# Layer 0 of a four-layer graph network: run sums as one product a block, the root on VectorE, end positions shifted by a product

## The chip, the cores and the metric

The kernel runs on one core of a Trainium2 chip. The metric is the device time of one execution in microseconds. A core has five engines: TensorE (PE; its weight loads are shown as PEld), VectorE (DVE), ScalarE (ACT), GpSimd (POOL) and SyncE (SP), which here only issues DMAs. Each engine runs its own instructions in order; between engines they wait on semaphores.

## What is computed

Four graph layers one after the other on 3125 nodes of 128 features and 103,125 edges, sorted by destination. The change touches the first, an attention over the edges of each destination node:

```python
q_dst = Q[dst] + rel_q[edge_type]
k_src = K[src] + rel_k[edge_type] + (time_emb @ Wt + bt)
v_src = V[src] + rel_v[edge_type]
euclid = sum(q_dst * k_src, axis=-1) / sqrt(DH)          # 8 heads of 16
decay = exp(decay_scale * tanh(relu(dec_in @ Wd1 + bd1) @ Wd2 + bd2))
man_dist = norm(m[src] - m[dst])                         # m: nodes mapped into a ball
logits = (alpha * euclid - (1 - alpha) * hyp_beta * man_dist) * decay
ex = exp(logits - segment_max(logits, dst)[dst])
agg = segment_sum(v_src * ex, dst) / segment_sum(ex, dst)
out = agg @ Wo + bo                                      # then norm, feed-forward, norm
```

## The kernel before

**Tiles and blocks.** Edges are cut into tiles of 128 and blocks of 8 tiles (`TPB`), 101 blocks (`NBLK`), 808 tiles (`TT`). One edge of a tile lies on each partition. Since edges are sorted by destination, a tile's edges fall into runs of equal destination. A node's edges may go on from one tile into the next.

**The layer-0 loop.** `sp_l0_windows`, `pool_l0_windows`, `act_l0_windows`, `dve_l0_windows` and `pe_l0_windows` are the five engines' programs of one software pipeline of `NBLK + 3` turns. In turn n they work on block n (loads, decay), block n-1 (scores and logits), block n-2 (run maxima, exponentials) and block n-3 (messages and sums). The order on each engine is written out by hand; semaphores of `Signals` (`g.…`) join them. A flag from the data (`all_near`) picks this path, since each block's destinations lie within 126 nodes (`WIN`).

**GpSimd** gathers the 128 source rows of 384 floats for each tile by indirect DMA (`pool_gather`, L1200) into a ring of four block buffers `GS`, eight gathers a block. For block n it first waits until `GS` of block n-4 is used (`gs_used`). Ahead of the seventh gather of turn n it takes the root of the squared distances of block n-2 (`pool_w_distances`, L1238): 128x8 elements to the power 0.5.

**SP** loads for each block the window of destination rows, the near keys, decay inputs, edge attributes, run rows (L916) and destination keys as two bf16 rows (L908), and stores the block's sums, 8 tiles x 128 rows x 144 floats, into `y_rows` (L921).

**TensorE** makes for each half block the attribute addend (L2451) and the picked destination rows (`pe_w_products`, L2459), turns logits into rows and back (L2479, L2495, L2496), spreads the keys over partitions (`pe_same_half`, L2420), and multiplies for each tile the matrix `same` (edge e and edge f have one destination) with the messages (`pe_sums`, L2443 and L2444), so that each of a tile's 128 rows holds its run's sum. In the trace an fp32 product is two records. The four pairs of a block's sums are spread over the turn. `pe_keep_busy` (L2434) makes three products of 128x512 into bank 0 that nothing reads.

**VectorE**, in its order: positions work (below), messages (L1870), scores of the first half (L1880, L1882, L1884), the decayed logits and two scans over runs (L1916 to L1922), `same` of the first half (L1854), scores of the second half, `same` of the second half, the head reduction (L1931), the window's low part (L1890), and then, after GpSimd's root (`dist_ready`), the logits (L1938 to L1940).

**ScalarE** makes the pick weights (L1411, L1418), the squares with their sums (L1394), the decay's functions, the exponentials, and copies the sums out of PSUM, four times 128x272 a block (L1380).

**End positions.** `dve_positions` finds for each node where its edges end, as a generator that is advanced once a turn: 25 turns with two 808-wide instructions each (L1823, L1824), then 25 turns in which GpSimd gathers a row of keys (a ninth gather) and VectorE counts in it (L1830, L1831). Then the end positions go to DRAM and come back shifted by one node, as start positions (`sp_positions`, L967 to L972, the third and fourth DMA column-wise in 4-byte pieces), for which VectorE waits at L1839.

**After the loop** `sp_join` loads the last row of each tile, `pool_join` gathers for each node the row of its last edge (`end_ix`) and the carry of its tile (`tile_ix`), and the join adds what earlier tiles hold of a node.

## Time and profile before

| | us |
|---|---|
| median of 3 runs | 4303.54 |
| lowest and highest of them | 4303.48 and 4307.41 |
| the profiled execution's own time | 4303.84 |
| its span, first to last instruction | 4302.1 |
| mean granted TensorE clock | 0.891 |

| engine | busy us | share of the span | instructions |
|---|---|---|---|
| TensorE products | 3349.1 | 78% | 31445 |
| TensorE weight loads | 2746.6 | 64% | 31445 |
| VectorE | 3220.5 | 75% | 6328 |
| ScalarE | 2083.6 | 48% | 6017 |
| GpSimd | 2220.2 | 52% | 2554 |

The layer-0 loop lies between about 190 and 1530 us of the span. The rest is the preparation ahead of it and the other three layers behind it, which the change leaves as they are. In the rows below a time is in us from the span's start; "mean ns" is that of one record; "[2.56 <-POOL …]" says how long the engine was idle before the instruction and what ended that. The share of busy time is an average over all layers; what a change in the loop is worth is read from the loop's own rows. The granted clock is given as a share of the full one, 2.4 GHz; the other level is 1.2 GHz.

### The profile page before, as it was taken

What the parts mean: (1) busy time and instruction counts of PE and PEld (TensorE: products, weight loads), DVE (VectorE), ACT (ScalarE), POOL (GpSimd) and SP (SyncE); (2) the same over time, 40 slices, a digit from 0 to 9 for tenths busy, and PEclk for the clock granted to TensorE, in tenths of its full rate; (3) what the DMA queues carried; (4) which work ended last, traced back from release to release, by engine and by line L of the source; (5) the groups of instructions that cost most, each with busy time, mean ns of one, the idle gap of its engine ahead of it and who ended that gap; (6) DMA issues with size and microseconds to landing.
All of it is one profiled execution on the core that took longest, in us unless ns stands there. A gap on an engine that the chain in (4) does not pass through costs nothing.

```text
span 4302.1 us, 86569 instructions
## 1 busy us (share of the span) xinstructions
PE 3349.1 (78%) x31445; PEld 2746.6 (64%) x31445; DVE 3220.5 (75%) x6328; ACT 2083.6 (48%) x6017; POOL 2220.2 (52%) x2554
## 2 busy tenths in 40 slices
PE   1389889879999936177856788857899999779995
PEld 1155555545555524177745678744899999679995
DVE  5488877767777734799957887767666666779997
ACT  2366655546666613499944576730322222234443
POOL 0277788858888750088822200000455555458883
PEclk7699999989999968588877899978999999989998
DMA  4677777778888720100002211123344444223331
GB/s 89 212 208 216 211 207 209 206 162 232 229 228 229 216 67 1 42 13 14 13 10 95 80 40 48 40 100 117 114 129 124 127 122 128 85 68 128 127 128 66
DMA packets 387384, 524.58 MB, mean 122 GB/s; under 512 B 85571, under 2 KB 315269, under 8 KB 386815
## 3 DMA queue, kind: packets, MB, share of 16 engines
q1 hardware_dynamic: 332799, 354.60, 27.8%
q0 software_dynamic: 54144, 164.25, 14.2%
q8 instruction: 258, 4.23, 0.4%
q14 instruction: 183, 1.50, 0.1%
HBM read 407.61 MB, written 111.07 MB: 121 GB/s over the span
## 4 chain that ended last, share of the span: by engine, by line
PE 33%; DVE 24%; POOL 21%; issue 11%; ACT 5%; DMA 4%; SPq 2%; DVEq 0%; POOLq 0%; ACTq 0%
POOL arena_a L1200 16%; PE psum L3726 5%; POOL arena_c L1238 4%; PE psum L3742 4%; PE psum L3677 4%; PE psum L3675 4%; PE psum L3642 2%; PE psum L3701 2%; PE psum L3724 2%; PE psum L3314 2%; DVE arena_a L3222 2%; PE psum L3673 2%; DVE arena_c L3215 1%; DVE msg_parts L3464 1%; DVE Hn L3192 1%
## 5 line engine op out<-in xcount | busy, mean ns | idle before, releaser
L1200 POOL DMA_INDIRECT arena_a<-src_table,src_tix x808 | 832.2, 1030 | 429.6 <-issue 387.8
L3446 POOL TENSOR_SCALAR node_hot<-arena_c 128x128 fp32r<-128x128 f32 x575 | 365.4, 646 | 903.3 <-DVE arena_c L3334 566.8
L3464 DVE SCALAR_TENSOR_TENSOR msg_parts<-psum,msg_parts 128x512 fp32r<-128x512 f32 (+2 forms) x644 | 425.6, 661 | 259.4 <-ACT msg_parts L3613 226.4
L3164 POOL TENSOR_SCALAR node_hot_dst<-arena_c 128x128 fp32r<-128x128 f32 x587 | 382.2, 667 | 123.9 <-DVE arena_c L3568 67.9
L3613 ACT ACTIVATE msg_parts<-psum 128x512 fp32r<-128x512 f32 (+2 forms) x325 | 186.2, 573 | 520.6 <-PE psum L3677 520.6
L3675 PE MATMUL psum<-arena_c,arena_a 128*128 128x128 bf16 x3675 | 406.4, 220 | 0.0
L3677 PE MATMUL psum<-arena_c,arena_a 128*128 128x128 bf16 x3675 | 406.4, 220 | 0.0
L1394 ACT ACTIVATE arena_a<-arena_a 128x128 f32<-128x128 f32 x808 | 239.2, 297 | 195.5 <-DVE arena_a L1882 195.3
L3673 PE MATMUL psum<-src_tix,arena_a 128*128 128x128 bf16 x1225 | 272.4, 222 | 71.0 <-DVE arena_a L3350 37.2
L3042 PE MATMUL psum<-arena_a,arena_c 128*128 128x150 f32 x1800 | 291.3, 329 | 39.9 <-ACT arena_c L2984 39.7
L3628 ACT ACTIVATE msg_parts<-psum 128x512 fp32r<-128x512 f32 (+1 forms) x319 | 185.2, 581 | 260.4 <-PE psum L3726 260.4
L3042 PEld LDWEIGHTS psum<-arena_a,arena_c 128*128 128x128 f32 x1800 | 280.5, 222 | 45.1 <-ACT arena_c L2984 43.8
L3726 PE MATMUL psum<-arena_c,arena_a 128*128 128x128 bf16 x3675 | 308.9, 219 | 0.0
L2434 PE MATMUL psum<-weights,ident 128*128 128x512 f32 x606 | 279.1, 597 | 0.1
L3314 PE MATMUL psum<-arena_a,arena_c 128*128 128x129 f32 x1250 | 201.1, 307 | 84.9 <-DVE arena_c L3215 84.8
L2981 ACT ACTIVATE arena_c<-arena_c,arena_b 128x128 f32<-128x128 f32 x850 | 251.1, 386 | 28.5 <-DVE arena_b L2895 28.5
L3675 PEld LDWEIGHTS psum<-arena_c,arena_a 128*128 128x128 bf16 x3675 | 258.1, 98 | 0.0
L1380 ACT ACTIVATE arena_c<-psum 128x272 f32<-128x272 f32 x404 | 157.5, 390 | 207.8 <-PE psum L2444 201.8
L3726 PEld LDWEIGHTS psum<-arena_c,arena_a 128*128 128x128 bf16 x3675 | 258.0, 98 | 0.0
L2443 PE MATMUL psum<-arena_c 128*128 128x136 f32 x808 | 186.8, 314 | 91.1 <-DVE arena_c L1870 91.0
L3677 PEld LDWEIGHTS psum<-arena_c,arena_a 128*128 128x128 bf16 x3675 | 257.7, 98 | 0.0
L2443 PEld LDWEIGHTS psum<-arena_c 128*128 128x128 f32 x808 | 135.7, 198 | 183.3 <-DVE arena_c L1870 111.4
(599 smaller groups left out, 10095.6 us busy)
## 6 DMA issues: line engine op xcount, KB each, us to landing
y_rows<-arena_c SPq DMA_DIRECT2D x101, 576.0 KB, 4.2
arena_a<-bucket_rows SPq DMA_DIRECT2D x150, 384.0 KB
arena_b<-near_keys SPq DMA_DIRECT2D x101, 252.0 KB
arena_a<-bucket_rows SPq DMA_DIRECT2D x50, 448.0 KB
arena_a<-bucket_lists SPq DMA_DIRECT2D x25, 896.0 KB
pair_counts<-arena_c SPq DMA_DIRECT2D x25, 800.0 KB
arena_a<-bucket_lists SPq DMA_DIRECT2D x25, 704.0 KB
arena_a<-src_table,src_tix POOLq DMA_INDIRECT x808
```

The lines of the kernel that those rows point to most:

```text
L1200: e.indirect_dma_start(out_, None, table, bass.IndirectOffsetOnAxis(ap=idx, axis=0)).then_inc(sem, 16)
L2434: e.matmul(bank[0][:, :], ident[:, :], Wt4[:, :], start=True, stop=True)
L2443: e.matmul(bank[bk][:, 0:w], same[s][:, t, :], msg[s][:, t, 0:w], start=True, stop=True)
L3042: put = e.matmul(bank[2 + s][:, 0:3 * KT], hot_pos[s][:, j, :], routed_v[s][:, j, :, :].rearrange("p f k -> p (f k)"), start=(j == 0), sto ...
L3164: return e.tensor_scalar(node_hot3[at % RING_H][:, i, :], iota_row, dst_lo[:, b, t:t + 1], None, ALU.is_equal)
L3314: put = e.matmul(bank[6 + b % 2][:, 0:D + 1], expd[b % 2][:, k, :], H1[:, k, :], start=(k == 0), stop=(k == NB - 1))
L3446: return e.tensor_scalar(node_hot[at % RING_M][:, i, :], iota_row, src_lo[:, b, 2 * k + j:2 * k + j + 1], None, ALU.is_equal)
L3464: e.scalar_tensor_tensor(out=to[:, 1, 0:nt, :], in0=bank[at % 4][:, 0:nt * P].rearrange("p (t f) -> p t f", f=P), scalar=0.0, in1=to[:, 0, ...
L3673: e.matmul(to, attr_rows[s][:, c_], Wc12, start=True, stop=False)
L3675: e.matmul(to, row_hot[0][s][:, c_], A3[:, part, sb_ * D:(sb_ + 1) * D], start=False, stop=False)
L3677: put = e.matmul(to, row_hot[1][s][:, c_], B3[:, part, b * D:(b + 1) * D], start=False, stop=(part == 2))
L3726: put = e.matmul(to, src_rows3[s][:, c_], A3[:, part, k * D:(k + 1) * D], start=False, stop=(part == 2))
```

## The change

- **Root.** `pool_w_distances` is gone from GpSimd. VectorE starts from a first guess taken from the bits of the number, and makes two Heron steps (guess + d2/guess) with two reciprocals, on 128x8 elements; its constants are folded into the next multiply. GpSimd's wait for a free ring buffer is now on the squares.
- **Run sums.** A block's nodes get rows by their number modulo 112 (`RES` = 128 - 16), so that a whole block's sums come from one accumulated product group: eight products of 128x144 into one bank (`pe_run_sums`), one copy out of PSUM (`act_run_sums`), and two stores (`sp_store_runs`), of 120 and of 8 rows of 144 floats. Rows 112 to 119 take the runs that carry over from an earlier tile (one for each tile), the last 8 rows the run at the end of each tile. The matrix for it (`dve_run_rows`) compares row numbers from `row_col` and `last_col`, made once ahead of the loop (`dve_run_columns`, with four products that shift the destination column by one partition or take its last one). The run's maximum goes in as 8 further columns, masked to the run's first edge (`first_col`). The key loads, `pe_same_half` and `dve_same_half` go from this loop.
- **End positions.** The shift by one node is a product with a rotated identity (`rotated`) and copies out of PSUM, instead of DMAs to DRAM and back. Index arithmetic for `run_ix` is added behind it. The gathers of end rows and the loads of last rows move into the loop's functions (`pool_end_rows`, `sp_last_rows`), behind the same waits.
- **Unread products.** `pe_keep_busy` is gone.
- The flag asks for a reach below 112 instead of 126 nodes, from the block's unclamped first key.

```diff
-                        e.wait_ge(g.dist_ready, n - RING + 1)
+                        e.wait_ge(g.squares, 2 * (n - RING + 1))
                     for t in range(TPB):
-                        if t == 3 * TPB // 4 and n >= 2:
-                            pool_w_distances(e, n - 2)
                         pool_gather(e, GS[n % RING][:, t, :], src0, src_tix[:, n * TPB + t:n * TPB + t + 1], g.d_gs[n % RING])
-                elif n - 2 < NBLK:
-                    pool_w_distances(e, n - 2)
+            pool_end_rows(e, 0, 1, 1, run_sums, run_ix)
...
+        def sp_store_runs(e, k):
+            s = k % 2
+            e.wait_ge(g.sums_out, 4 * (k + 1))
+            e.dma_start(run_sums[k * RES_ALL:(k + 1) * RES_ALL, :], sums_w[s][0:RES_ALL, :]).then_inc(g.d_y[s], 16)
+            e.dma_start(last_sums[k * TPB:(k + 1) * TPB, :], sums_w[s][RES_ALL:P, :]).then_inc(g.d_last[s], 16)
...
+        def act_run_sums(e, k):
+            s = k % 2
+            e.wait_ge(g.sums_pe, 4 * (k + 1))
+            if k >= 2:
+                e.wait_ge(g.d_y[s], 16 * (k // 2))
+                e.wait_ge(g.d_last[s], 16 * (k // 2))
+            e.activation(sums_w[s], bank[SUM_BANKS_W[s]][:, 0:WMAX], ACT.Copy).then_inc(g.sums_out, 4)
...
         def dve_l0_messages(e, k):
             s, r = k % 2, k % RING
             e.wait_ge(g.exp_ready, k + 1)
+            e.wait_ge(g.max_copied, k + 1)
             if k >= 2:
                 e.wait_ge(g.sums_pe, 4 * (k - 1))
-            e.tensor_tensor(msg[s][:, :, 0:D].rearrange("p t (h w) -> p t h w", h=H),
+            e.tensor_tensor(msg_w[s][:, :, D + H:D + 2 * H], v3(max_w[s]), bc(first_col[:, k * TPB:(k + 1) * TPB], 2, H), ALU.mult)
+            e.tensor_tensor(msg_w[s][:, :, 0:D].rearrange("p t (h w) -> p t h w", h=H),
...
+        def dve_run_rows(e, k):
+            s = k % 2
+            if k >= 2:
+                e.wait_ge(g.sums_pe, 4 * (k - 1))
+            at = slice(k * TPB, (k + 1) * TPB)
+            e.tensor_tensor(same[s][:, :, 0:RES_ALL], bc(row_col[:, at], 2, RES_ALL), bc(row_no_w[:, 0:RES_ALL], 1, TPB), ALU.is_equal)
+            e.tensor_tensor(same[s][:, :, RES_ALL:P], bc(last_col[:, at], 2, TPB), bc(row_no_w[:, RES_ALL:P], 1, TPB), ALU.is_equal).then_inc(g.same_ready, 2)
...
-                    dve_same_half(e, i2, 0, dst_col, 0)
+                    dve_run_rows(e, i2)
                 if b1:
                     dve_w_scores(e, i1, 1)
-                if b2:
-                    dve_same_half(e, i2, 1, dst_col, 0)
-                if b1:
                     eu, d2, lg, t1 = small[s1][:, 0, :], small[s1][:, 1, 0:TPB], small[s1][:, 3, :], small[s1][:, 4, :]
                     e.wait_ge(g.q_used, 2 * i1 + 2)
                     own.mark(e.tensor_reduce(v3(eu), GS[i1 % RING][:, :, 0:D].rearrange("p t (h w) -> p t h w", h=H), AX, ALU.add))
+                    guess, other = small[s1][:, 1, TPB:2 * TPB], small[s1][:, 1, 2 * TPB:3 * TPB]
+                    e.wait_ge(g.squares, 2 * i1 + 2)
+                    own.step(e.tensor_scalar(guess.bitcast(I32), d2.bitcast(I32), 0.5, ROOT_BITS, ALU.mult, ALU.add))
+                    own.mark(e.reciprocal(other, guess))
                 if b0:
                     dve_w_low(e, i0)
                 if b1:
-                    e.wait_ge(g.dist_ready, i1 + 1)
+                    own.settle()
+                    own.mark(e.tensor_tensor(other, other, d2, ALU.mult))
+                    own.mark(e.tensor_tensor(v3(eu), v3(eu), bc(hrow[:, 1, :], 1, TPB), ALU.mult))
+                    own.settle()
+                    own.step(e.tensor_tensor(guess, guess, other, ALU.add))
+                    own.step(e.reciprocal(other, guess))
+                    own.step(e.tensor_tensor(other, other, d2, ALU.mult))
+                    own.step(e.scalar_tensor_tensor(out=guess, in0=guess, scalar=0.25 * ROOT_TRIM ** 2, in1=other, op0=ALU.mult, op1=ALU.add))
                     if i1 >= 2:
                         e.wait_ge(g.rows_pe, i1 - 1)
-                    own.step(e.tensor_tensor(v3(t1), bc(d2, 2, H), bc(hrow[:, 2, :], 1, TPB), ALU.mult))
-                    own.step(e.tensor_tensor(v3(eu), v3(eu), bc(hrow[:, 1, :], 1, TPB), ALU.mult))
+                    own.step(e.scalar_tensor_tensor(out=v3(t1), in0=bc(guess, 2, H), scalar=1.0 / ROOT_TRIM, in1=bc(hrow[:, 2, :], 1, TPB), op0=ALU.mult, op1=ALU.mult))
                     e.tensor_tensor(lg, eu, t1, ALU.subtract).then_inc(g.logits_ready, 1)
...
-        def pe_keep_busy(e, k):
-
-            e.wait_ge(g.addend_used, 2 * k + 2)
-            for _ in range(3):
-                e.matmul(bank[0][:, :], ident[:, :], Wt4[:, :], start=True, stop=True)
-
...
+        def pe_run_sums(e, k):
+            s = k % 2
+            e.wait_ge(g.gs_used, k + 1)
+            e.wait_ge(g.same_ready, 2 * (k + 1))
+            if k >= 2:
+                e.wait_ge(g.sums_out, 4 * (k - 1))
+            for t in range(TPB):
+                rows = e.matmul(bank[SUM_BANKS_W[s]][:, 0:WMAX], same[s][:, t, :], msg_w[s][:, t, :], start=(t == 0), stop=(t == TPB - 1))
+            rows.then_inc(g.sums_pe, 4)
...
                 if b3:
-                    e.wait_ge(g.gs_used, i3 + 1)
-                    pe_sums(e, i3, D + H, 0, 0, SUM_BANKS_W)
+                    pe_run_sums(e, i3)
...
+                if n == 2 * NB + 1:
+                    e.wait_ge(g.pos_ends, 1)
+                    e.matmul(bank[2][:, 0:NB], keys_pos[True][1], end, start=True, stop=True).then_inc(g.d_pos, 48)
```

## Rows read from the trace of the kernel before

**Rows 1.** Chain of waits by line, 1000 to 1030 us, steady part.

```profile
by line: POOL arena_a L1200 64.3%; issue 27.8%; POOL arena_c L1238 11.2%
```

**Rows 2.** Stretches: length, power instruction's busy (count), clock, DMA share, GB/s.

```profile
209.90:521.40 311.50, 43.30 (x24) 0.96 0.76 210
521.40:868.40 347.00, 41.91 (x25) 0.91 0.74 206
868.40:946.40 78.00, 6.67 (x4) 0.74 0.71 144
946.40:1495.30 548.90, 75.33 (x45) 1.00 0.81 228
```

**Rows 3.** Timeline, GpSimd: start, duration us, operation [idle before <- releaser].

```profile
1007.26 1.67 POOL L1238 TENSOR_TENSOR arena_c<-arena_c,weights 128x8 f32<-128x8 f32 x1
1009.11 1.02 POOL L1200 DMA_INDIRECT arena_a<-src_table,src_tix  x1 [0.18 <-issue]
...
1011.97 0.95 POOL L1200 DMA_INDIRECT arena_a<-src_table,src_tix  x1 [0.30 <-issue]
```

**Rows 4.** Timeline, VectorE, same window: parts of one block.

```profile
1008.97 0.23 DVE L1938 TENSOR_TENSOR arena_c<-arena_c,hrow 128x64 f32<-128x64 f32 x1 [2.56 <-POOL arena_c L1238]
1009.48 0.22 DVE L1940 TENSOR_TENSOR arena_c<-arena_c 128x64 f32<-128x64 f32 x1
1009.63 1.22 DVE L1870 TENSOR_TENSOR arena_c<-arena_a,arena_c 128x1024 f32<-128x1024 f32 x1
1010.76 0.68 DVE L1880 TENSOR_TENSOR arena_a<-arena_a,psum 128x512 f32<-128x512 f32 x1
...
1012.55 0.28 DVE L1916 TENSOR_TENSOR arena_c<-psum,arena_c 64x128 f32<-64x128 f32 x1
...
1014.16 0.68 DVE L1854 TENSOR_TENSOR arena_c<-psum,dst_col 128x512 f32<-128x512 f32 x1
```

**Rows 5.** VectorE's waits, 872 to 945: us, times, longest us.

```profile
DVE npos L1839 <- DMA npos<-end_pos: 12.5, 1, 12.5
DVE arena_c L1916 <- DMA arena_c<-run_rows: 12.5, 2, 12.3
```

**Rows 6.** Timeline, VectorE, before the loop: 25-wide waited steps.

```profile
44.67 0.18 DVE L1711 TENSOR_SCALAR stat<-stat 128x25 f32<-128x25 f32 x1
44.88 0.31 DVE L1712 RECIPROCAL stat<-stat 128x25 f32<-128x25 f32 x1
```

**Rows 7.** Groups by line, VectorE, 211 to 520: busy us, mean ns.

```profile
L1824 DVE TENSOR_REDUCE npos<-arena_b 128x1 f32<-128x808 f32 x24 | 23.9, 995 | 0.8
L1823 DVE TENSOR_SCALAR arena_b<-dst_tix,node_id 128x808 f32<-128x808 f32 x24 | 15.2, 633 | 0.0
```

**Rows 8.** Stretch before the loop: length, VectorE busy (count), clock, DMA.

```profile
176.20:191.50 15.30, 0.00 (x0) 0.50 0.79 213
```

**Rows 9.** The page's groups by line: busy us, mean ns, idle before.

```profile
L2434 PE MATMUL psum<-weights,ident 128*128 128x512 f32 x606 | 279.1, 597 | 0.1
```

**Rows 10.** One block: PE, PEld, DVE, ACT, POOL busy (counts), clock, DMA.

```profile
1009.60:1021.90 12.30, 11.45 (x58) 7.27 (x56) 9.57 (x20) 8.12 (x30) 9.97 (x10) 1.00 0.80 227
```

**Rows 11.** Chain of waits at the loop's end: start us, us, what.

```profile
1524.11 0.45 PE psum L2443 x2
...
1529.09 4.62 DMA y_rows<-arena_c
```

**Rows 12.** Timeline, TensorE, at three places in order of time.

```profile
306.36 0.50 PE L2443 MATMUL psum<-arena_c 128*128 128x136 f32 x2 [1.72 <-DVE arena_c L1870]
...
941.27 2.69 PE L2459 MATMUL psum<-win_parts_last,pick_w_last 128*128 128x256 f32 x8
...
1010.90 0.50 PE L2443 MATMUL psum<-arena_c 128*128 128x136 f32 x2 [0.82 <-DVE arena_c L1870]
...
1012.10 1.12 PE L2451 MATMUL psum<-weights,arena_c 128*128 128x512 f32 x2
1012.78 1.40 PE L2459 MATMUL psum<-win_parts_last,pick_w_last 128*128 128x256 f32 x8
```

More of the change, by code:

```diff
@@ L54 @@
 WIN = P - NET
+RES = P - 2 * TPB
+RES_ALL = RES + TPB
+ROUND = 8388608.0
 def bc(ap, axis, n):
@@ L502, in program @@
         tlog = [c_.take(4 * P, TPB * H).rearrange("p (t f) -> p t f", t=4) for _ in range(2)]
+        runs_at = 2 * TPB * P
+        w_at = runs_at + 2 * TPB * WMAX
+        flat_c = lambda at, n: arena_c[:, at:at + n]
+        msg_w = [flat_c(runs_at + s * TPB * WMAX, TPB * WMAX).rearrange("p (t f) -> p t f", t=TPB) for s in range(2)]
+        sums_w = [flat_c(w_at + s * WMAX, WMAX) for s in range(2)]
+        row_col, last_col, first_col = (flat_c(w_at + 2 * WMAX + i * TT, TT) for i in range(3))
+        row_no_w = flat_c(w_at + 2 * WMAX + 3 * TT, P)
+        max_w = [flat_c(w_at + 2 * WMAX + 3 * TT + P + s * TPB * H, TPB * H) for s in range(2)]
+        shift_w, final_w = same[0][:, 0, :], same[0][:, 1, :]
+        no_edge = same[0][:, 2, 0:1]
+        run_t = [flat_c(TPB * P, TT), flat_c(runs_at, TT), flat_c(runs_at + TT, TT)]
         RING_IX = 3
@@ L963, in sp_positions @@
             e.dma_start(last_row, row_bc(first_last[1, 0:TT])).then_inc(g.d_pos, 16)
+            if near:
+                return
             for _ in range(2 * NB + 2):
@@ L1838, in dve_positions @@
             e.wait_ge(g.d_pos, 80)
+            if near:
+                e.wait_ge(g.pos_ends, 1)
+                own.mark(e.tensor_copy(start[:, 1:NB], bank[2][:, 1:NB]))
+                own.step(e.tensor_copy(start[:, 0:1], bank[2][:, 0:1]))
+                own.mark(e.tensor_copy(start[0:1, 1:NB], bank[2][0:1, 0:NB - 1]))
+                own.step(e.memset(start[0:1, 0:1], 0.0))
             own.step(e.tensor_tensor(degree, end, start, ALU.subtract))
@@ L1846, in dve_positions @@
             own.step(e.tensor_tensor(has_carry, has_carry, valid, ALU.mult))
+            if not near:
+                return
+            own.mark(e.tensor_scalar(run_ix[:, :], tile_ix[:, :], 3, None, ALU.arith_shift_right))
+            own.step(e.tensor_scalar(lastp, node_id[:, :], 1.0 / RES, 0.5 / RES - 0.5, ALU.mult, ALU.add))
+            own.mark(e.tensor_copy(cnt, run_ix[:, :]))
+            own.step(e.tensor_scalar(lastp, lastp, ROUND, None, ALU.add))
+            own.step(e.tensor_scalar(lastp, lastp, -ROUND, None, ALU.add))
+            own.mark(e.scalar_tensor_tensor(out=start, in0=cnt, scalar=-float(TPB), in1=te, op0=ALU.mult, op1=ALU.add))
+            own.step(e.scalar_tensor_tensor(out=lastp, in0=lastp, scalar=-float(RES), in1=node_id[:, :], op0=ALU.mult, op1=ALU.add))
+            own.step(e.scalar_tensor_tensor(out=start, in0=start, scalar=float(RES), in1=lastp, op0=ALU.add, op1=ALU.subtract))
+            own.step(e.tensor_tensor(start, start, has_carry, ALU.mult))
+            own.step(e.tensor_tensor(lastp, lastp, start, ALU.add))
+            own.step(e.scalar_tensor_tensor(out=run_ix[:, :], in0=cnt, scalar=float(RES_ALL), in1=lastp, op0=ALU.mult, op1=ALU.add))
         def dve_same_half(e, k, hf, key_col, layers):
@@ L1895, in dve_l0_windows @@
             e.tensor_tensor(minus_place, minus_place, iota_col, ALU.subtract)
-            e.memset(half_row, 0.5)
             e.memset(wd2_wide, 0.0)
+            e.memset(shift_w[:, 0:1], 0.0)
+            e.tensor_copy(shift_w[:, 1:P], ident[:, 0:P - 1])
+            e.tensor_scalar(final_w, ones[:, :], ident[:, P - 1:P], None, ALU.mult)
+            own.mark(e.tensor_scalar(no_edge, ident[:, 0:1], -5.0, None, ALU.mult))
             e.memset(wd1_2, 0.0).then_inc(g.l0_prep, 1)
+            dve_run_columns(e, own)
             positions = dve_positions(e, own, True)
@@ L2464, in pe_l0_windows @@
             rows_ = bank[3][0:R, 0:P]
+            e.wait_ge(g.l0_prep, 2)
+            for i, (lo, hi) in enumerate(((0, HALF), (HALF, TT))):
+                e.matmul(bank[1 + 6 * i][:, 0:hi - lo], shift_w, dst_col[:, lo:hi], start=True, stop=True)
+                columns = e.matmul(bank[2 + 4 * i][:, 0:hi - lo], final_w, dst_col[:, lo:hi], start=True, stop=True)
+            columns.then_inc(g.keys_read, 2 * NBLK)
             e.wait_ge(g.d_dec, 192)
```

108 lines of the change are left out of this document (66 added, 42 removed).

## The prediction

> **What bounds the kernel now.** I read the views in this order: the chain of waits, the layer-0 loop in stretches, then one block of it on each engine. In the steady part of the loop the chain lies on GpSimd alone: gathers of source rows, the issue gaps between them, and the power instruction [rows 1]. The loop goes through four stretches, cut at the starts of that instruction: 24 blocks in 311.5 us (12.98 each), 25 in 347.0 (13.88), 4 in 78.0 (19.5), 45 in 548.9 (12.20) [rows 2]. In the last, GpSimd never waits for another engine; the power instruction takes 1.67 us and the next gather starts 0.18 after it, where a gather follows a gather after 0.30 [rows 3]. VectorE meanwhile stands idle 2.56 us before L1938, waiting for it [rows 4]. In the 24 blocks VectorE also does two 808-wide instructions for the end positions, in the 25 GpSimd does a ninth gather. In the 4 blocks VectorE waits 12.5 us for the start positions that come back from DRAM and 12.5 for a load of run rows queued on SP behind them [rows 5].
>
> **GpSimd.** Without the power instruction a block loses 1.67 + 0.18 - 0.30 = 1.55 us: its floor falls to 12.20 - 1.55 = 10.65, and to 13.88 - 1.55 = 12.33 where it has nine gathers. The ring of four buffers gives a gather about two block times, so it isn't what binds. The gathers of end rows only move to another function, same place in the queue. One small iota is put ahead of the first gather: at most 1 us, in GpSimd's slack while VectorE is late.
>
> **VectorE** is next late, so its block must be priced, in start-to-start steps [rows 4]. A 1024-wide instruction costs 1.13, a 64-wide one 0.15, or 0.26 if the next waits for it (0.51 for two). The block is then: the new masked maximum, 64 wide, 0.15; messages 1.13; scores of the first half 1.79; the scans 1.61; the new comparison for the whole block, 960 and 64 elements, 1.06 + 0.15 = 1.21 in place of two of 512 (0.60 each); scores of the second half 1.79; reduction 1.13. That is 8.81. The root comes on top. A 25-wide step with a wait costs 0.21, a reciprocal 0.35 [rows 6]; for 8 elements I take 0.20 and 0.25. First guess 0.20, reciprocal 0.13 (the window's low part runs in its shadow, 256 wide and so between the 64 and the 512: 0.33), product and scaled score 0.35, then add, reciprocal, product, weighted sum 0.20 + 0.25 + 0.20 + 0.20, the two 64-wide ones 0.25 + 0.15. With the low part that is 2.26, so 11.07 a block. The bounds of the root: 0.5 less if waits hide in each other, and 0.9 more if each of its seven waited steps costs the 0.35 of a reciprocal. It now waits for ScalarE's squares where GpSimd did; behind the wait stand the guess, the low part and the logits, and TensorE's next picks wait for the low part. The second multiply and the reduction (0.60 + 1.13) lie between, so I take 0, at most 0.5. In the 24 blocks the position work adds 0.63 + 1.00 and two gaps [rows 7], 1.70, so 12.77; in the 25, two 128-wide ones, about 0.5, so 11.57, under GpSimd's 12.33.
>
> Before the loop about 18 VectorE instructions of 400 to 808 elements and four products are added. At 0.65 to 1.0 us each and some 6 us for the products they take about 13 us, inside a stretch of 15.3 us in which VectorE does nothing [rows 8]. I take 0; if that cover were short, the overrun counts in full, 5 us at most.
>
> **TensorE.** Removed per block: the three unread products (L2434, 279.1 us over 101 blocks, 2.76 each [rows 9]) and the two key products. The engine was busy 11.45 of 12.30 [rows 10], so it is left with about 8 of 11 to 13 us. The other edit is in the order. The sums were spread, one pair ahead of the second half's picks; now all eight stand ahead of them. From the end of the messages at full clock: eight products at 0.23 (half of the 0.45 that one takes at the low clock [rows 11]) and 0.1 to start, 1.94; the hidden product about 0.3; the addend 0.68 and the picks 1.40 [rows 12]. Ready after 4.3 us. VectorE wants them after 1.79 + 1.61 + 1.21 + 0.60 = 5.2, so 0.9 is left. At the low clock it is 3.7 (eight at 0.45 and the start) + 0.5 + 1.36 (twice 0.68) + 2.69 [rows 12] = 8.25: VectorE then stalls 3.0 us.
>
> The granted clock therefore decides the size. In the steady stretch TensorE waits 0.82 us a block for the messages and stays at 1.00, which is 2.4 GHz; with 1.7 us of waiting the mean is 0.96 [rows 2, 12], so some time passes at 1.2 GHz. After the change it idles from the end of its decay and addend products, some 9.2 us after a block's low part, until the next low part at 11.1, and again until the messages are done: 1.9 + 1.0 us, in the 24 blocks 1.9 + 2.8. I expect a low spell in most blocks, over part of the sums and picks only, since the engine is full again once they run: 3.6 us of them in the 24 blocks, where it idles longest, 2.4 otherwise (estimates). A low spell costs half its length, 1.8 and 1.2. Less the 0.9 this leaves a stall of about 0.9 us in the 24 blocks, 0.3 later; bounds 0 and 3.0.
>
> The Trainium skill speaks against the change here ("TensorE: Matmul & The Clock Gate", section "HAM oscillation — how this bites in real kernels"): a loop whose TensorE waits in each turn can lose the high clock in each turn. Were every block's second half run at the low clock, it would give the slower rival below instead of the forecast.
>
> **ScalarE and DMA.** Four evictions of 272 columns become one of 144; the store of 576 KB a block becomes 74 KB in two issues, the 4 KB key load goes. Nothing waited for these in the steady stretch, so 0. ScalarE's new wait, for the block's sums, ends about 2 us after the messages and holds back the squares of the second half, which can't start for another 4: 0.
>
> **End positions.** The round trip through DRAM goes, for one product, two copies and some 15 steps of 25 elements (about 4.5 us with the index arithmetic). The 4 blocks become 4 x 11.37 + 4.5 = 50.
>
> **The end.** The last sums are one run instead of four, and the last store and its landing (4.62 us [rows 11]) shrink: I take 6 us, between 2 and 9.
>
> **The sum**, against the profiled execution's own 4303.84 us (its span is 4302.1; the median of the three runs is 4303.54, 0.3 less, which I neglect):
> 24 x (12.77 + 0.9) = 328.1, +16.6; 25 x 12.33 = 308.3, -38.7; 50 for 78, -28.0; 45 x (11.07 + 0.3) = 511.7, -37.2; the end -6. Together -93.3: **4210 us**.
>
> **Rivals.**
> - *The clock holds.* The gaps are short, as is the 0.82 at full clock [rows 12]. Stalls 0: 24 x -0.21, -39, -29, 45 x -1.13, -6, that is -130: 4174. If moreover GpSimd's gathers drop to the 0.95 + 0.30 of a plain one [rows 3], the nine-gather stretch falls to 11.57: 4155.
> - *The root is dear.* 0.9 us more on 98 blocks, less what GpSimd covers in the 25: about +65, 4275. For it: each step is a round trip on one engine. Against: [rows 6].
> - *TensorE binds, slower.* The low clock covers the stretch from the sums to the second picks in most blocks. With a mean stall s above 0.74 us the sum is -149 + 98 s; it turns slower at s = 1.5, half of the 3.0. With s = 2.0: +47, 4351. For it: the unread products are gone and the sums now stand in front. Against: a busy stretch brings the clock back, since the 1.00 of the steady stretch followed a stretch of 0.74 [rows 2].
> - *The cover is elsewhere*: VectorE's growth eats what GpSimd gives up (11.07 + 1.1 a block), only the round trip stays: about -5 to +10, 4305.
>
> **How the numbers follow.** Forecast 0.5 (4180 to 4245), clock holds 0.22, dear root 0.13, TensorE binds 0.08, no gain 0.05, below all 0.02. The range takes the first three with the root's upper bound: 4150 to 4285. Faster by over 0.2% (8.6 us, about what a measurement can tell from no change): 0.87; within 0.04; slower 0.09.
>
> **What would show it.** No power instruction; VectorE's idle before L1938's successor gone and VectorE at 95% or more of the loop; block times near 13.7, 12.3 and 11.4; TensorE's clock in the last stretch below 1.00, with VectorE's waits in front of the second half's subtraction naming the picks; no wait for end_pos. The prediction is wrong if the waited 8-wide steps aren't near 0.20, if the low clock covers all or none of the sums, or if the work before the loop sticks out of its 15.3 us.

## The result, and the profile after

The changed kernel takes 4260.4 us (median of 4 runs, 4251.7 to 4263.3), the kernel before beside it 4305.5 (4 runs, 4303.5 to 4309.7): a ratio of 0.9891, interval 0.9873 to 0.9908, 45 us or 1.1% faster. The forecast was 4210, 93 us faster. The sign is right, less than half of the size came. Submitted again later on another chip (after_again, below), it took 4262.6 us in three of five executions; the other two, 4354.5 and 4356.4 us, fell in a slower state that some executions show, and count in no ratio here.

The page of the changed kernel, its span, parts 1 and 2 (engines, clock and DMA in 40 slices), the engines' shares of the chain, and two of the groups by line:

```profile
span 4261.3 us, 84541 instructions
PE 3127.8 (73%) x30647; PEld 2694.0 (63%) x30647; DVE 3368.9 (79%) x7173; ACT 1961.6 (46%) x5714; POOL 2053.6 (48%) x2454
...
POOL 0355567776666440288813200000555555368883
PEclk7688889899999857688867899978999999889998
DMA  4755566666666410100012211133444444223331
...
PE 42%; DVE 41%; issue 7%; ACT 5%; DMA 3%; SPq 2%; POOL 1%; DVEq 0%; ACTq 0%; POOLq 0%
...
L1232 POOL DMA_INDIRECT arena_a<-src_table,src_tix x808 | 829.9, 1027 | 411.8 <-issue 224.9
...
L2567 PE MATMUL psum<-arena_c 128*128 128x144 f32 x1616 | 327.8, 378 | 156.1 <-DVE arena_c L1926 156.1
```

The power instruction is gone, and with it GpSimd's place in the chain of waits (1%): it now waits for VectorE to free a ring buffer. These shares are of the whole span, all four layers. Of the chain between 210 and 520 us alone the run sums (L2567) take 27%: TensorE now bounds a part of this loop. The loop's four stretches, as columns us, then PE, PEld, DVE, ACT and POOL busy, granted clock, DMA share and GB/s, and what VectorE waits for in the loop:

```profile
210.00:520.00 310.00, 223.86 (x1021) 165.85 (x1020) 271.98 (x625) 145.93 (x558) 165.32 (x168) 0.82 0.55 155
520.00:835.00 315.00, 236.98 (x1174) 172.17 (x1173) 284.05 (x708) 167.10 (x638) 235.12 (x213) 0.88 0.62 177
835.00:880.00 45.00, 33.21 (x167) 24.86 (x166) 41.30 (x108) 23.12 (x88) 35.25 (x33) 0.89 0.65 190
880.00:1430.00 550.00, 421.55 (x2246) 307.08 (x2246) 513.14 (x1286) 321.59 (x1214) 376.97 (x378) 0.94 0.68 194
```

```profile
DVE arena_a L1971 <- PE psum L2549: 59.5, 61, 2.1
DVE arena_a L1973 <- PE psum L2557: 11.5, 60, 0.2
```

Where GpSimd held VectorE up, by 2.56 us in the block of [rows 4], TensorE now does in 61 of the 101 blocks: L1971 adds the addend product (L2549), L1973 subtracts the picks (L2557), both behind the run sums (L2567) in TensorE's order. The clock is 0.82 in the first stretch, 0.94 in the last; it was 0.96 and 1.00 [rows 2]. One block of the first stretch, first TensorE, then VectorE, as start us, us, operation [idle before <- releaser]:

```profile
310.36 4.21 PE L2567 MATMUL psum<-arena_c 128*128 128x144 f32 x16 [2.66 <-DVE arena_c L1926]
314.51 0.60 PE L2598 MATMUL psum<-arena_c,arena_b 24*128 24x512 bf16 x1
315.04 1.86 PE L2549 MATMUL psum<-weights,arena_c 128*128 128x512 f32 x2
316.13 1.72 PE L2557 MATMUL psum<-win_parts_last,pick_w_last 128*128 128x256 f32 x8
```

```profile
309.09 1.22 DVE L1926 TENSOR_TENSOR arena_c<-arena_a,arena_c 128x1024 f32<-128x1024 f32 x1
...
317.01 0.69 DVE L1971 TENSOR_TENSOR arena_a<-arena_a,psum 128x512 f32<-128x512 f32 x1 [2.09 <-PE psum L2549]
317.88 0.69 DVE L1973 TENSOR_TENSOR arena_a<-arena_a,psum 128x512 f32<-128x512 f32 x1 [0.19 <-PE psum L2557]
```

TensorE idles 2.66 us for the messages and then runs the eight sums in 4.21 us at the low level (a product of fp32 data is two records). Each of the first 23 blocks is longer than the 12.93 us that the experiments below show for VectorE without waits: they take 13.7 to 15.4. In the last stretch the same group of sums is longer or shorter from block to block; where it is short, 2.23 us, VectorE doesn't wait. There 27 of 45 blocks take 11.2 us and 18 take 12.0 to 12.4:

```profile
1207.70 3.75 PE L2567 MATMUL psum<-arena_c 128*128 128x144 f32 x16 [0.95 <-DVE arena_c L1926]
...
1219.86 2.23 PE L2567 MATMUL psum<-arena_c 128*128 128x144 f32 x16 [0.95 <-DVE arena_c L1926]
```

From start to start of the messages (L1870 before, L1926 after), by the timelines; the forecast counted 24, 25, 4 and 45 blocks:

| part of the loop | before, us | after, us | difference | forecast |
|---|---|---|---|---|
| 23 blocks with position work | 299.8 | 332.8 | +33.0 | +16.6 |
| 25 with nine gathers | 346.0 | 318.0 | -28.0 | -38.7 |
| 5 of the middle | 89.3 | 63.8 | -25.5 | -28.0 |
| 45 full blocks | 546.9 | 525.3 | -21.6 | -37.2 |
| ahead, last 2 blocks, end, rest | | | +1.3 | -6 |

Together -40.8, the difference of the two spans.

### The profile page after: what moved, and what is told of

Read it like the earlier page. It is cut to its first block, busy times and chain, and to the rows that moved or that the text cites. A ratio compares the mean times of both kernels' runs of the same rounds, so it can differ in the third digit from the quotient of the medians.

```text
span 4261.3 us, 84541 instructions
## 1 busy us (share of the span) xinstructions
PE 3127.8 (73%) x30647; PEld 2694.0 (63%) x30647; DVE 3368.9 (79%) x7173; ACT 1961.6 (46%) x5714; POOL 2053.6 (48%) x2454
## 4 chain that ended last, share of the span: by engine, by line
PE 42%; DVE 41%; issue 7%; ACT 5%; DMA 3%; SPq 2%; POOL 1%; DVEq 0%; ACTq 0%; POOLq 0%
PE psum L2567 6%; PE psum L3830 5%; PE psum L3846 4%; PE psum L3781 4%; PE psum L3779 4%; DVE arena_c L2025 3%; DVE arena_c L1926 3%; PE psum L3746 2%; DVE arena_a L1975 2%; PE psum L3805 2%; PE psum L2549 2%; DVE arena_a L3326 2%; PE psum L3828 2%; PE psum L3418 2%; DVE arena_a L1973 2%
## 5 line engine op out<-in xcount | busy, mean ns | idle before, releaser
L2567 PE MATMUL psum<-arena_c 128*128 128x144 f32 x1616 | 327.8, 378 | 156.1 <-DVE arena_c L1926 156.1
L2567 PEld LDWEIGHTS psum<-arena_c 128*128 128x128 f32 x1616 | 301.4, 265 | 175.5 <-DVE arena_c L1926 175.5
L3777 PE MATMUL psum<-src_tix,arena_a 128*128 128x128 bf16 x1225 | 272.4, 222 | 70.9 <-DVE arena_a L3454 37.2
L3418 PE MATMUL psum<-arena_a,arena_c 128*128 128x129 f32 x1250 | 202.6, 309 | 89.4 <-DVE arena_c L3319 89.3
L2557 PEld LDWEIGHTS psum<-win_parts,pick_w 128*128 128x128 f32 x1088 | 145.5, 191 | 166.5 <-DVE win_parts L1981 130.6
L2557 PE MATMUL psum<-win_parts,pick_w 128*128 128x256 f32 x1088 | 188.0, 315 | 75.3 <-DVE win_parts L1981 75.1
```

Of the source, the lines that this page charges most:

```text
L2557: rows = e.matmul(picked[:, t, :], pick_w[s][:, 4 * hf + t, :], win_parts[s][:, part, :], start=(part == 0), stop=(part == 1))
L2567: rows = e.matmul(bank[SUM_BANKS_W[s]][:, 0:WMAX], same[s][:, t, :], msg_w[s][:, t, :], start=(t == 0), stop=(t == TPB - 1))
L3418: put = e.matmul(bank[6 + b % 2][:, 0:D + 1], expd[b % 2][:, k, :], H1[:, k, :], start=(k == 0), stop=(k == NB - 1))
L3777: e.matmul(to, attr_rows[s][:, c_], Wc12, start=True, stop=False)
```

## Experiments

### Does the stall need the low clock and the sums in front, both?

The theory: VectorE is held up only where TensorE is at its lower level *and* has the run sums in front of what VectorE waits for. Then taking either away is enough. The rival: VectorE's block is as long as it is for other reasons, and neither helps. **busy_back** puts the three unread products back into the changed kernel, ahead of the decay products:

```
+            e.wait_ge(g.addend_used, 2 * k + 2)
+            for _ in range(3):
+                e.matmul(bank[0][:, :], ident[:, :], Wt4[:, :], start=True, stop=True)
```

> The changed kernel with the three unread products put back, ahead of the decay products. Theory (the low clock stretches the sums and picks, and VectorE stalls on them): granted clock of the last stretch back to 0.99 or more, VectorE's waits for the addend and the picks from 71 us to under 10, block times 12.9 in the first 23 intervals (now 14.5), 12.0 to 12.4 in the next 25 (now 12.7), 11.2 in the last 45 (now 11.7); 4180 to 4200 us. Rival (the order alone: eight products ahead of the second half's picks are too many at any clock, and 2.8 us more of TensorE work makes it later): block times as they are or longer, 4260 to 4290 us.

**sums_late** leaves TensorE's work as it is and moves it: the sums stand behind the second half's picks, ScalarE's copy of them behind the exponentials' copies.

```
-                if b3:
-                    pe_run_sums(e, i3)
                 if b1:
                     pe_w_products(e, i1, 1)
+                if b3:
+                    pe_run_sums(e, i3)
```

> The changed kernel with the sums of a block behind the second half's picks instead of ahead of them (their copy out of PSUM moves behind the exponentials on ScalarE). Theory (it takes both, the low clock and the place of the sums): the clock stays at 0.8 to 0.95, but VectorE's waits for the addend and picks fall from 71 us to under 20, 4190 to 4215 us. Rival (whatever the order, a loop at the low clock is TensorE's): waits only move to the first half's picks, 4245 to 4270 us.

**both** does the two together, and **before_idle** only takes the three unread products out of the kernel before:

```
                 if b1:
-                    pe_keep_busy(e, i1)
```

> Both edits together: sums behind the picks, unread products back. If each of them alone removes the stall, the two give no more than the better one, 4180 to 4200 us, bounded by VectorE's 11.2 us and GpSimd's nine gathers. If each removes a part, this one is clearly below both.

> The kernel before without the three unread products, nothing else. Theory: the clock of the loop falls below 0.95 here too, but its sums are spread and VectorE has 1.6 to 3.8 us of idle time before the root in each block, so little of it reaches the end: 4300 to 4330 us. Rival (the low spells of the changed kernel come from something else, such as its shorter sums): the clock stays near 0.98 and the time at 4304.

The kernel before took 4311.0 us beside them. busy_back: 4197.8, ratio 0.9735 (0.9719 to 0.9752). sums_late: 4200.8, 0.9744 (0.9727 to 0.9762). both: 4202.2, 0.9748 (0.9730 to 0.9766). before_idle: 4318.6, 1.0017 (1.0008 to 1.0027). The stretches of busy_back, then of sums_late (columns as above):

```profile
210.00:520.00 310.00, 257.24 (x1281) 167.09 (x1280) 299.29 (x698) 169.09 (x624) 189.38 (x185) 1.00 0.61 172
880.00:1400.00 520.00, 500.00 (x2500) 326.13 (x2500) 502.48 (x1252) 322.24 (x1203) 361.89 (x364) 1.00 0.69 198
```

```profile
210.00:520.00 310.00, 237.03 (x1138) 176.90 (x1137) 299.29 (x696) 165.94 (x623) 190.25 (x186) 0.82 0.61 172
880.00:1400.00 520.00, 421.97 (x2224) 304.19 (x2222) 502.44 (x1256) 314.57 (x1200) 399.94 (x364) 0.91 0.70 198
```

VectorE's busy time is the same to 0.04 us, with the clock at 1.00 in one and at 0.82 and 0.91 in the other. All that sums_late's VectorE still waits for between 210 and 1400 us is a gather of position keys; in busy_back it is that (14.5 us) and TensorE in three blocks:

```profile
DVE arena_b L1861 <- DMA arena_b<-dst_keys,end_ix: 16.8, 16, 1.4
```

```profile
DVE arena_a L1971 <- PE psum L2549: 3.4, 3, 2.1
DVE arena_a L1973 <- PE psum L2557: 0.6, 3, 0.2
```

Their blocks are the same too: 12.93 and 12.94 in the first stretch, 12.49 and 12.52 in the second, 11.22 and 11.23 in the last, against 14.47, 12.72 and 11.67 in the changed kernel. So the low clock alone costs nothing, nor does the order alone; the two together cost about 60 us (58.6 between after_again and busy_back_2 below, on one chip). both adds nothing, since there is only one stall to remove. In the kernel before, the unread products were worth 8 us, nearly all of it in the first 23 blocks (299.8 to 306.9 us without them): there GpSimd hid most of what the low clock does (clock 0.81 to 0.84 without them).

### What each part earned

These alter sums_late, so that no stall blurs them. Its 4201 us are their control, from another chip: root_back_3 ran on one more, the other two on a third, and the kernel before took 4311, 4308 and 4305 us on the three. **root_back_3** gives the root to GpSimd's power instruction again, after the sixth gather as before. **ends_back_3** takes the start positions through DRAM again. **one_step_3** leaves out the second Heron step (the root is less exact; 0.57 us of VectorE a block):

```
-                    own.step(e.reciprocal(other, guess))
-                    own.step(e.tensor_tensor(other, other, d2, ALU.mult))
-                    own.step(e.scalar_tensor_tensor(out=guess, in0=guess, scalar=0.25 * ROOT_TRIM ** 2, in1=other, ...))
```

The first two, where they differ most from sums_late:

```
                     for t in range(TPB):
+                        if t == 3 * TPB // 4 and n >= 2:
+                            pool_w_distances(e, n - 2)
...
+            e.tensor_tensor(d2, d2, half_row, ALU.pow).then_inc(g.dist_ready, 1)
```

```
-                if n == 2 * NB + 1:
-                    e.wait_ge(g.pos_ends, 1)
-                    e.matmul(bank[2][:, 0:NB], keys_pos[True][1], end, start=True, stop=True).then_inc(g.d_pos, 48)
```

> sums_late with the root by GpSimd's power again. On a chip where the kernel before takes 4305 to 4315 us: 4200 + 45 x 1.2 + 48 x 0.4 = about 4275 us if the power and its gap set GpSimd's block, under 4230 if most of the gain is that of the sums. On a chip where the kernel before takes about 4400: 0.98 to 0.99 of it again.

> sums_late with the start positions taken through memory again. If the product earned what the middle stretch lost in the changed kernel (89.3 to 63.8 us), this takes 4200 + 26 = about 4226 us, 0.981 of the kernel before. If the round trip costs nothing beside a faster loop, 0.974.

> sums_late with one Heron step in place of two (0.57 us a block left out, so the root is less exact). If VectorE sets the last 45 full blocks, they go from 11.23 to about 10.7 us, which is also the eight gathers of a block (10.1 to 10.7), and the time from 4200 to about 4175 us, 0.969 of the kernel before. If something else sets them, it stays at 0.974. If it is 1.00, as on the two chips before, it is a matter of the order of the waits and not of the chip.

root_back_3 took 4333.0 us beside 4308.5 of the kernel before, ratio 1.0057 (1.0040 to 1.0074): *slower* than the kernel before, with all other parts of the change in it, and 58 us above the 4275 that I expected. ends_back_3 took 4225.6 beside 4304.9, 0.9811 (0.9790 to 0.9833), as forecast: VectorE waits for end_pos again,

```profile
DVE npos L1868 <- DMA npos<-end_pos: 14.5, 1, 14.5
```

and the five middle blocks take 86.3 us. one_step_3 took 4196.3 beside 4304.9, 0.9750 (0.9733 to 0.9767): of the 25 us that I expected, 5 at most came. Its first 53 blocks are faster (12.23, 12.34 and 11.42 us each), the last 45 slower, 11.76 against 11.23.

Two of these need a cause: why root_back_3's blocks, which GpSimd bounds as in the kernel before, take 12.76 us in the last stretch and 14.54 with nine gathers, where the kernel before took 12.15 and 13.84; and why less VectorE work makes the last stretch longer. Both are in the gathers. root_back_3's timeline, GpSimd and then VectorE:

```profile
1202.21 1.02 POOL L1233 DMA_INDIRECT arena_a<-src_table,src_tix  x1 [0.18 <-issue]
1203.54 1.37 POOL L1233 DMA_INDIRECT arena_a<-src_table,src_tix  x1 [0.30 <-issue]
1205.21 0.96 POOL L1233 DMA_INDIRECT arena_a<-src_table,src_tix  x1 [0.30 <-issue]
1206.48 1.12 POOL L1233 DMA_INDIRECT arena_a<-src_table,src_tix  x1 [0.30 <-issue]
1207.90 1.47 POOL L1233 DMA_INDIRECT arena_a<-src_table,src_tix  x1 [0.30 <-issue]
```

```profile
1202.86 1.22 DVE L1938 TENSOR_TENSOR arena_c<-arena_a,arena_c 128x1024 f32<-128x1024 f32 x1
...
1207.39 1.14 DVE L1947 TENSOR_TENSOR arena_c<-arena_c 128x960 f32<-128x960 f32 x1
```

Two gathers of a block are long: the one that runs into the messages (L1938) and the one that runs into the run rows' comparison (L1947). Each ends 0.83 or 0.84 us after VectorE's instruction does (1204.91 and 1204.08, 1209.37 and 1208.53). Both instructions read both operands from SBUF; beside those that read one from PSUM a gather takes 0.95. The traces of six kernels (before, after, busy_back, sums_late, root_back_3, one_step_3; 215 to 1380 us) show no exception: all 764 gathers that start while one of these two instructions runs end 0.81 to 0.85 us after it, and the 650 that had started 0.3 us or more ahead of it keep 0.94 to 1.15 us. Over 900 to 1380 us I counted gathers longer than 1.2 us: 36 of 297 in the kernel before (one a block), 74 of 299 in root_back_3 (two a block), 86 of 343 in sums_late. What all gathers of that stretch take above 0.95 us each comes to 21.0, 43.4 and 51.4 us. The kernel before compared its keys with a PSUM bank (L1854), so it had one such instruction; the new comparison is the second. That is 0.6 us a block of GpSimd that the forecast didn't have, and it is what root_back_3's last blocks are longer by. It costs sums_late no time, but there too it is all that GpSimd had to spare: from 900 to 1380 us GpSimd has no gap above 0.35 us, so neither engine has slack at 11.23 us a block, while in busy_back it waits 45 times for VectorE in the last stretch (880 to 1400 us). What GpSimd waits for VectorE between 210 and 1400 us (us, times, longest), sums_late and then busy_back:

```profile
POOL arena_a L1232 <- DVE arena_c L1926: 69.5, 23, 12.8
POOL arena_a L1232 <- DVE arena_c L1926: 123.1, 69, 13.4
```

No run puts an operand in PSUM back into the comparison, so this cause rests on the timing. The Trainium skill has such a contention in "SBUF — State Buffer", section "Who interferes with whom": a VectorE instruction with two SBUF inputs contends with a GpSimd instruction that reads SBUF, because its second input comes through a read interface that the two engines share. The trace agrees: the gather reads its indices from SBUF, and where it starts while such an instruction runs it ends 0.81 to 0.85 us after it, as above.

In one_step_3 many of the long gathers fall at the beginning of the instruction and wait it out in full (GpSimd, then VectorE):

```profile
1101.84 1.89 POOL L1232 DMA_INDIRECT arena_a<-src_table,src_tix  x1 [0.30 <-issue]
...
1119.37 2.04 POOL L1232 DMA_INDIRECT arena_a<-src_table,src_tix  x1 [0.30 <-issue]
```

```profile
1101.70 1.22 DVE L1926 TENSOR_TENSOR arena_c<-arena_a,arena_c 128x1024 f32<-128x1024 f32 x1
1103.90 0.69 DVE L1971 TENSOR_TENSOR arena_a<-arena_a,psum 128x512 f32<-128x512 f32 x1 [0.98 <-DMA arena_a<-src_table,src_tix]
...
1119.45 1.14 DVE L1935 TENSOR_TENSOR arena_c<-arena_c 128x960 f32<-128x960 f32 x1
```

VectorE then waits for the gathers (51.9 us in 40 waits) and goes on as they land: 77 long ones of 326, and 72.3 us above 0.95 each in all, where sums_late had 51.4. The blocks vary from 10.5 to 12.5 us; GpSimd, again without a gap above 0.35 us, bounds them. Its floor isn't a number of its own; it depends on where VectorE's instructions fall against the gathers. That the shorter VectorE work moved them there is what the two traces show side by side; no run moved them and nothing else.

### The same kernels on two other chips

Four kernels ran first on a chip on which the kernel before took 4408 us, and the control with three of them again on one on which it took 4380. No number above is from there.

> The version with the sums behind the picks, the root back on GpSimd as a power instruction (and its wait on VectorE). Theory (that version's loop is VectorE's, 11.2 us a block, and GpSimd's floor with the root is 12.2 and 13.8): block times 13.0, 13.8 and 12.15 again, VectorE idle before the logits; 4199 + 0 to 5 + 25 x 1.3 + 45 x 0.93 = 4275 us, 4265 to 4285. Rival (the root's place is worth little, the gain is in the shorter sums and comparisons): below 4225 us.

> The version with the sums behind the picks, with one Heron step instead of two; this leaves out the second refinement of the root, so the distances are about a thousandth off. It takes away four waited 8-wide steps, 0.2 to 0.24 us each. Theory (VectorE binds all through): the unstalled block falls from 11.2 to 10.4 by VectorE, so GpSimd's 10.65 binds in the last 45; 12.1 in the first 23; about 4199 - 18 - 25 - 0 to 5 = 4155 us. Rival (waits hide in one another): less than half of it, 4180 us or more.

> The version with the sums behind the picks, with the start positions through DRAM again instead of the product. Theory (the round trip costs what the trace of before shows, two stalls of VectorE of 12.5 us, and SP's queue): the 5 intervals around it go from 61 to 85 to 90 us; 4222 to 4230 us. Rival (with a VectorE that binds, the wait is hidden or SP's backlog costs more later): under 4210 or over 4245.

> The changed kernel (sums ahead of the picks) with one unread product a block put back instead of three. Theory (the granted clock follows how little TensorE idles in a stretch, and the stall follows the clock): the clock lies between 0.94 and 1.00 in the last stretch, the waits between 71 us and 6, the time between 4198 and 4260, about 4225 us. If one is as good as three, 4198; if the three act in another way than by the clock, the clock and the time don't move together.

> The same kernel as sums_late (the changed kernel with the run sums behind the second half's picks), as the control of this group: the four runs before this one came from a chip on which the kernel before took 4408 us and not 4311, and where three kernels built on this order took 4333 to 4430. If the spread belongs to the chip, this kernel is at 0.974 of the kernel before wherever the kernel before takes 4305 to 4315, with no wait of ScalarE ahead of the copies of the transposed maxima (L1490). If it belongs to the kernels, the control is at 0.974 even where the kernel before takes about 4400, and only the altered kernels show that wait.

root_back took 4333.1 us, ratio 0.981 (0.976 to 0.987), one_step 4400.8, 0.999 (0.996 to 1.002), ends_back 4429.8, 1.005 (1.002 to 1.008), and busy_one, the changed kernel with one unread product (three lines of busy_back with range(1)), 4519.9, 1.025 (1.018 to 1.031). On the other chip the control sums_late_2 took 4385.4 us, 1.002 (1.000 to 1.004), one_step_2 4377.9, 1.001 (0.998 to 1.005), ends_back_2 4412.1, 1.007 (1.005 to 1.010), and root_back_2 4330.5, 0.988 (0.984 to 0.991).

> sums_late with one Heron step in place of two (a reciprocal and two 8-wide steps, 0.57 us a block, left out, so the root is less exact). If VectorE sets the block wherever GpSimd does not, the 45 full blocks go from 11.23 to about 10.7 us: 4200 - 45 x 0.55 = about 4175 us, and some 10 us less again from the 53 blocks ahead of them, which are GpSimd's at 12.5 to 12.9. If the freed VectorE only lets another engine bind, nothing is gained (4200) or the block is longer than the control's, and the trace names the engine that VectorE then waits for.

> sums_late with the start positions taken through memory again, as in the kernel before. If the shift by a product earned the 28 us that the five blocks of the middle stretch lost less (89.3 to 63.8 us), this takes 4200 + 26 = about 4226 us, with two waits of about 12.5 us of VectorE on loads. If the round trip was hidden by the gathers of the ring, it takes 4200.

> sums_late with the root by GpSimd's power again. If GpSimd's 1.67 us power and its 0.18 us gap set the block of the last 45, that block is 12.5 us against the control's 11.23, and the first 48 gain nothing from their gathers being alone: 4200 + 45 x 1.2 + 48 x 0.4 = about 4275 us. If most of the gain came from the sums and not from the root, it stays under 4230.

The same kernel is 0.974 on one chip and 1.002, in all ten executions, on another, so the difference goes with the chip and not with the altered parts. busy_one ran there alone, so it doesn't say how many unread products the changed kernel needs. The trace of sums_late_2 has a wait that no trace above has: what ScalarE waits for in the loop (us, times, longest), and VectorE's timeline just ahead of it:

```profile
ACT arena_c L1490 <- remote: 393.1, 81, 7.7
```

```profile
204.15 0.69 DVE L1971 TENSOR_TENSOR arena_a<-arena_a,psum 128x512 f32<-128x512 f32 x1 [0.16 <-issue]
213.78 0.69 DVE L1973 TENSOR_TENSOR arena_a<-arena_a,psum 128x512 f32<-128x512 f32 x1 [8.95 <-remote]
```

In the code both wait for TensorE: L1490 for its transposes, L1973 for its picks, and by the records TensorE had done them 4.5 us (at one L1490, 1021.08) and 8.5 us (at this L1973) earlier. In sums_late the L1490 wait is 10.1 us in all. So the signal, or the work that the record shows as done, comes late there. Why stays open. root_back took 4330 to 4333 on all three chips. That its VectorE waits for GpSimd in most blocks anyway doesn't explain it: so does the kernel before, and that one is 1.7 to 2.4% slower there.

A last group asked whether the main results hold on a fourth chip, with the kernel before at 4308.5:

> The changed kernel, unchanged. On a chip where the kernel before takes 4305 to 4315 us: 0.989 of it. On a chip where it takes about 4400: if the root on VectorE is what those chips charge (root_back was 0.981 and 0.988 there, its control 1.002), this kernel is slower than the kernel before, 1.00 to 1.03; if they charge the late place of the sums, it is at 0.98 to 0.99 there too.

> The changed kernel with the three unread products back. On a chip where the kernel before takes 4305 to 4315 us: 0.974 of it, as before. On a chip where it takes about 4400: with one unread product it was 1.025 there, so with three 1.00 to 1.05 if TensorE's amount of work is what those chips charge, and 0.974 if only the single product's kernel was odd.

after_again took 4262.6 us, ratio 0.9885 (0.9865 to 0.9906), busy_back_2 4204.0, 0.9755 (0.9738 to 0.9773): both as at first. The kernel before submitted once more took 4310.6, 1.0003 (0.9992 to 1.0013), and its trace has one such wait, of 0.6 us. Whether the change earns anything on the two slower chips wasn't measured.

## Why the prediction fell short

**What bounds it.** Right for GpSimd and VectorE: with the power instruction gone VectorE is next late. root_back_3 shows that without the root's move the other parts bring nothing together (1.0057): what the end positions earn there (66.0 us for the five middle blocks instead of 89.3), the longer gathers take back.

**VectorE's block.** Forecast 11.07, measured 11.22 where it doesn't wait (busy_back). The root in one block, VectorE's timeline of the changed kernel: 8-wide steps start 0.20 to 0.24 us after one another, and the low part (L1981) lies in the shadow of the first reciprocal:

```profile
1204.00 0.21 DVE L2028 TENSOR_SCALAR arena_c<-arena_c 128x8 int32<-128x8 int32 x1
1204.25 0.20 DVE L2029 RECIPROCAL arena_c<-arena_c 128x8 f32<-128x8 f32 x1
1204.37 0.38 DVE L1981 TENSOR_TENSOR win_parts<-arena_b,win_parts 128x256 fp32r<-128x256 f32 x1
...
1205.19 0.20 DVE L2038 RECIPROCAL arena_c<-arena_c 128x8 f32<-128x8 f32 x1
1205.43 0.17 DVE L2039 TENSOR_TENSOR arena_c<-arena_c 128x8 f32<-128x8 f32 x1
1205.63 0.17 DVE L2040 SCALAR_TENSOR_TENSOR arena_c<-arena_c 128x8 f32<-128x8 f32 x1
1205.83 0.29 DVE L2043 SCALAR_TENSOR_TENSOR arena_c<-arena_c,hrow 128x64 f32<-128x64 f32 x1
```

From the guess's start to the masked maximum's (1206.29) that is 2.29 us, forecast 2.26. The rival *The root is dear* is out. The first stretch is 12.93 without waits, forecast 12.77.

**TensorE: the step that failed.** The mechanism was right: the slack of 0.9 us, the wait at the second half, the low spell. What failed is the size of one term, the low spell of 3.6 us in the first stretch. The granted clock of 0.82 over 310 us is 112 us at the low level (310 x 0.18 x 2), 5.2 us for each block. In the block shown it covers the sums (4.21 us, 2.23 where the clock is full), the hidden product (0.60 as against 0.38) and part of the addend (1.86 as against 1.12), and so the stall is 2.09 us. The 3.6 was an estimate with no row behind it, and it leaned on "the engine is full again once they run"; here the engine worked through all of the sums before its products were short again.

In the last stretch I expected a low spell of 2.4 us in most blocks; the clock of 0.94 gives 1.4 us a block (550 x 0.06 x 2 over 47), but they are not spread: 18 of 45 blocks are held up by about 1 us, 27 not at all. Of the 71 us that VectorE waits for TensorE, 59.5 are for the addend, which it wants first, and not for the picks that the prediction named as the sign.

The sums were also priced too low: eight and the start were to take 1.94 and 3.7 us, they take 2.23 and 4.21. From start to start a product takes 0.245 and 0.48 us, not 0.23 and 0.45: 6% more for 6% more columns (144, and 136 in [rows 11]); the rest is the first record and the end of the last.

Mean stall of the first stretch 14.47 - 12.93 = 1.54 us, forecast 0.9: 15 of the 16.4 us that are missing there. In the last, 11.67 - 11.22 = 0.45, forecast 0.3: 7 us, and the block's 0.15 another 7 of the missing 15.6. The rule of the Trainium skill that I set against the change ("TensorE: Matmul & The Clock Gate", section "HAM oscillation — how this bites in real kernels") holds in the first stretch, where all 23 blocks are held up at a mean clock of 0.82, and in part in the last. That section's example waits 3 to 5 us in each turn; here idle times of 0.90, 0.40 and 2.66 us in a block went with it. I gave the outcome that it would have 0.08 and should have let it move the forecast itself.

**GpSimd's floor.** Forecast 12.33 with nine gathers; without the stall it is 12.5, with it 12.72: 10 us short. The floor was taken as the old block less the power instruction, as if the gathers wouldn't notice what VectorE runs beside them: from 530 to 830 us they take 21 us above 0.95 each in the kernel before, and 35 us in busy_back. The 10.65 of the last stretch wasn't tested in the change, since VectorE's 11.2 is longer; in one_step_3, where VectorE needed less, it wasn't reached (11.76).

**The clock holds** (4174) is what busy_back comes nearest to, at 4197.8: the forecast of that rival lacked 0.15 us of VectorE, 0.15 of the nine-gather block, and most of the 6 us of the end.

**End positions.** Right: -25.5 for -28.0. ends_back_3 is 24.8 us slower than sums_late, and its five middle blocks take 86.3 us, sums_late's 60.8. **Before the loop**: the first messages start 2.0 us earlier than before, so the 15.3 us [rows 8] did cover what was added. **The end**: from the last messages to the join's first product 12.1 us against 13.8, so 1.7 us gained, not 6: in the chains at the end the last store's landing went from 4.62 us [rows 11] to 3.41 and no further, and the load behind it from 3.12 to 3.53. The unchanged code behind it took 3 us more, which I don't explain.

Better than the change as it stands is the changed kernel with the sums behind the picks (4200.8 us), or with the unread products kept (4197.8): 2.6% faster than the kernel before, twice and more what the change brings.

## What to carry to other kernels

When the engine that bounds a loop is relieved, price the order of the others at the *lower* clock: put work that the waiting engine doesn't need behind what it does need; here the level then didn't matter. Unread products that keep the clock up and a better order are two cures of the same stall; test one with the other in place before taking either out. A floor read off one engine's own durations holds only as long as its neighbour's instructions stay the same.

## What the runs showed of the hardware

- A gather issued by GpSimd that starts while VectorE runs a 960- or 1024-wide product or comparison with both operands in SBUF ends 0.81 to 0.85 us after that instruction, wherever in it it began: 0.95 us alone, up to 2.0 beside one. Started 0.3 us or more ahead, it isn't held. Beside instructions that read PSUM it stays at 0.95.
- Shorter VectorE work made the last stretch longer (11.23 to 11.76 us a block), with the gathers' time above 0.95 us each going from 51.4 to 72.3 us.
- fp32 products accumulated over eight weights, 144 columns: 0.245 us from start to start at full granted clock, 0.48 at the low one; the group of eight 2.23 and 4.21 us.
- At a mean granted clock of 0.82 to 0.91 the kernel took the same time as at 1.00 (4200.8 and 4197.8 us) once the run sums stood behind what VectorE waits for.
- On two chips of five the kernel before took 4380 to 4408 us and not 4305 to 4311; on the one of them that ran it the control was 4% slower, with waits that ended 4.5 and 8.5 us after TensorE's recorded end.
